# A message-passing kernel on one core: VectorE's edge loop written out for every iteration, and one wait per slot on GpSimd

## What is computed

```python
h = jnp.maximum(_layernorm(x), 0.0)
# node side: 32 scalars and 32 vectors of 3 per node, two small linear maps
sc_s, sc_v = fctp(x_s, x_v, sc_ws, sc_wv, MUL)
l1_s, l1_v = fctp(x_s, x_v, lin1_ws, lin1_wv, MUL)
# edge side
h = silu(rbf(d) @ fc_w1 / sqrt(8)); h = silu(h @ fc_w2 / 8)
w00, w01, w10, w11 = split(h @ fc_w3 / 8, 4)
gs, gv = l1_s[edge_src], l1_v[edge_src]          # the gather
o00 = w00 * gs * sh0;  o01 = w01 * gs * sh1
o10 = w10 * gv * sh0;  o11 = w11 * (gv . sh1) / sqrt(3)
agg = segment_sum(concat(...), edge_dst) / count  # the scatter
out = x + sc + tanh(agg_s @ alpha_w * ...) * lin2(agg)
```

## Time and profile before

| what | us |
|---|---|
| median of 3 runs | 2520.62 |
| lowest, highest | 2513.36, 2520.88 |
| span of the profiled execution | 2483.8 |
| time of the profiled execution itself | not given beside its span |
| PE busy | 1811.4 (73%) |
| DVE (VectorE) busy | 1783.0 (72%) |
| POOL (GpSimd) busy | 1578.4 (64%) |
| ACT (ScalarE) busy | 1199.1 (48%) |

### The profile page before, as it was taken

How to read it: one execution, slowest core, us unless ns; L and a number is a source line. 1 busy time by engine, 2 the same in 40 slices (tenths; PEclk the granted TensorE clock), 3 DMA queues, 4 the chain that set the end, 5 groups by cost and what they waited for, 6 DMA issues and landing times. The chain is left out here.

```text
span 2483.8 us, 34021 instructions
## 1 busy us (share of the span) xinstructions
PE 1811.4 (73%) x7969; PEld 1174.2 (47%) x7969; DVE 1783.0 (72%) x4669; ACT 1199.1 (48%) x3310; POOL 1578.4 (64%) x1624
## 2 busy tenths in 40 slices
PE   6577777787777777767677767667787776877777
PEld 6344444454444444444444434444554444544544
DVE  8577767767776777767676667767677776777777
ACT  6354545455454555444444344445444444445443
POOL 7566666666666666666666666666666666666563
PEclk9588878878888887788787878888888888888889
DMA  7322222222222222222122222222222222222222
GB/s 214 70 64 67 56 64 66 66 56 66 66 59 62 67 65 56 55 48 50 46 50 48 48 48 49 54 50 64 57 67 62 59 65 66 53 64 61 59 66 55
DMA packets 347699, 155.73 MB, mean 63 GB/s; under 512 B 237983, under 2 KB 322048, under 8 KB 347584
## 3 DMA queue, kind: packets, MB, share of 16 engines
q0 software_dynamic: 50016, 102.51, 15.7%
q1 hardware_dynamic: 296938, 51.75, 11.4%
q10 hardware_dynamic: 630, 0.29, 0.0%
HBM read 134.27 MB, written 20.15 MB: 62 GB/s over the span
## 5 line engine op out<-in xcount | busy, mean ns | idle before, releaser
L970 POOL DMA_INDIRECT lin_g<-lin_table,src_ix x1563 | 1530.0, 979 | 865.1 <-issue 441.5
L1157 ACT ACTIVATE lin_sh<-lin_g,harm 128x128 f32<-128x128 f32 x1563 | 483.8, 396 | 94.6 <-DMA lin_g<-lin_table,src_ix 87.6
L1040 PE MATMUL ps_sums<-near_sums,far_hot 128*128 128x257 f32 x520 | 208.0, 488 | 440.8 <-DVE agg L1474 206.0
L1030 PE MATMUL ps_near<-msg,onehot 128*64 128x257 f32 x3126 | 507.5, 471 | 1.2 <-DVE msg L1423 1.2
L1018 PE MATMUL ps_w<-w,h 128*128 128x256 f32 x1566 | 462.6, 440 | 28.2 <-ACT key_all L1167 18.5
L1018 PEld LDWEIGHTS ps_w<-w,h 128*128 128x128 f32 x1566 | 395.3, 272 | 135.4 <-issue 44.9
L999 PE MATMUL ps_h<-rbf,w 32*128 32x192 f32 x1044 | 277.0, 390 | 138.0 <-issue 67.1
L1415 DVE TENSOR_TENSOR msg<-lin_sh,key_all 128x576 f32<-128x576 f32 (+1 forms) x261 | 197.3, 756 | 249.9 <-ACT key_all L1167 209.5
L1167 ACT ACTIVATE key_all<-ps_w 128x768 f32<-128x768 f32 x261 | 213.5, 818 | 305.2 <-remote 188.6
L1030 PEld LDWEIGHTS ps_near<-msg,onehot 128*64 128x64 f32 x3126 | 241.3, 164 | 230.6 <-issue 175.7
L1383 DVE TENSOR_TENSOR lin_sh<-lin_g,ps_meta 128x576 f32<-128x576 f32 (+1 forms) x261 | 196.6, 753 | 212.2 <-DMA lin_g<-lin_table,src_ix 207.0
(11 more groups left out here) (175 smaller groups left out, 1655.2 us busy)
## 6 DMA issues: line engine op xcount, KB each, us to landing
lin_g<-lin_table,src_ix POOLq DMA_INDIRECT x1563
dist_in<-in_edge_weight SPq DMA_DIRECT2D x67, 96.0 KB
lin_table<-lin_out SPq DMA_DIRECT2D x24, 256.0 KB, 2.6
x_in<-in_x SPq DMA_DIRECT2D x24, 256.0 KB
skip_table<-x_in SPq DMA_DIRECT2D x24, 256.0 KB
xq<-in_x SPq DMA_DIRECT2D x23, 256.0 KB, 3.9
harm<-in_edge_attr SPq DMA_DIRECT2D x66, 48.0 KB
x_in<-skip_table SPq DMA_DIRECT2D x8, 256.0 KB
```

Source lines behind the costliest of these rows:

```text
L970: pool.indirect_dma_start(slot_tiles(s, u)[rows, t, :], None, lin_table, bass.IndirectOffsetOnAxis(ap=src_ix[rows, s.phase, u, col:col + 1 ...
L1030: mm = pe.matmul(ps_near[half * NEAR:(half + 1) * NEAR, 0:MSG + 1], onehot[:, u, t, :], msg[:, u % 2, t, :], start=(j == 0), stop=(j == PA ...
L1040: pe.matmul(ps_nodes(i), far_hot[:, u, :], near_sums[:, u % 2, :], start=True, stop=True).then_inc(sums_ready, 1)
L1157: last = act.activation(lin_sh0[:, u % 2, j, :], slot_tiles(s, u)[:, j, :], ACT.Copy, scale=harm[:, s.phase, u, harm_col(j):harm_col(j) + 1])
```

## The change

Two things. On VectorE the three hardware loops go; every iteration is written out with its number as a constant. Where the code told iteration 0 from the others by "the number is a constant", it now asks for the number 0. On GpSimd the three waits inside a group's gathers go; in their place is one wait before tile 0, for `msg_ready` of group n-4: VectorE has finished the message of the group that used the slot.

```diff
+            def first_turn(i):
+                return isinstance(i, int) and i == 0
...
-                return [(b, REST_ROWS[b]) for b in range(REST)] if isinstance(i, int) else [(b, P) for b in range(NB)]
+                return [(b, REST_ROWS[b]) for b in range(REST)] if first_turn(i) else [(b, P) for b in range(NB)]
...
-                                pool.wait_ge(near_ready, s.i * SLOTS + u - SLOTS + 1)
+                                pool.wait_ge(msg_ready, s.i * SLOTS + u - SLOTS + 1)
                                 pool.nop(nofuse=True)
...
-                            for k, t in enumerate(tiles):
-                                if not first and k == 2:
-                                    pool.wait_ge(h2_done, s.i * SLOTS + u)
-                                    pool.nop(nofuse=True)
-                                if not first and k == 4:
-                                    pool.wait_ge(sums_ready, s.i * SLOTS + u - SLOTS + 1)
-                                    pool.nop(nofuse=True)
+                            for t in tiles:
...
                         body(turn_of(0), share=True)
-                        with dve.Fori(0, STEPS // RING) as t:
-                            for k in range(RING):
-                                body(turn_in(t, 1, k), share=True)
-                        with dve.Fori(0, PLAIN // RING) as t:
-                            for k in range(RING):
-                                body(turn_in(t, 1 + STEPS, k))
-                        for i in range(1 + STEPS + PLAIN, EARLY0):
+                        for i in range(1, 1 + STEPS):
+                            body(turn_of(i), share=True)
+                        for i in range(1 + STEPS, EARLY0):
                             body(turn_of(i))
-                        body(turn_of(EARLY0), early=True)
-                        with dve.Fori(0, (EARLY - 1) // RING) as t:
-                            for k in range(RING):
-                                body(turn_in(t, EARLY0 + 1, k), early=True, finish=True)
+                        for i in range(EARLY0, ITERS - 1):
+                            body(turn_of(i), early=True, finish=i > EARLY0)
                         body(turn_of(ITERS - 1), finish=True, last=True)
```

More of the change, by code:

```diff
@@ L789, in gnn_kernel @@
             SKIP_STORES = 16 * (REST + STEPS)
+            def first_turn(i):
+                return isinstance(i, int) and i == 0
             def skip_rows(i):
-                return [(b, REST_ROWS[b]) for b in range(REST)] if isinstance(i, int) else [(b, P) for b in range(NB)]
+                return [(b, REST_ROWS[b]) for b in range(REST)] if first_turn(i) else [(b, P) for b in range(NB)]
             def skip_block(i, b):
-                return STEPS * NB + b if isinstance(i, int) else i * NB + (b - NB)
+                return STEPS * NB + b if first_turn(i) else i * NB + (b - NB)
             KEY_STEPS = HALVES
@@ L1459, in skip_sum @@
                             dve.wait_ge(sc_scaled, i + 1)
-                            for b, rows in skip_rows(i) if isinstance(i, int) else ():
+                            for b, rows in skip_rows(i) if first_turn(i) else ():
                                 last = dve.tensor_tensor(x_in[0:rows, b, :], ps_skip[0:rows, b * P:(b + 1) * P], x_in[0:rows, b, :], ALU.add)
-                            if not isinstance(i, int):
+                            if not first_turn(i):
                                 last = dve.tensor_tensor(x_in[:].rearrange("p b d -> p (b d)"), ps_skip[:], x_in[:].rearrange("p b d -> p (b d)"), ALU.add)
```

## The result

The changed kernel takes 2798.93 us (median of 4 runs, 2790.13 to 2799.64) against 2516.99 us: the ratio is 1.1114, with a 95% interval of 1.1088 to 1.114. The prediction was slower, 2595 us in a range up to 2770. The sign held, the size did not.

What follows compares the result with a forecast made beforehand. Waits were taken to bound the kernel: TensorE's signals held while GpSimd gathers. Span 2483.8 - 20 (loop) + 82 (longer stops) = 2546, plus 36.8 gives 2583, plus 13 for short cycles: 2595 us; range 2350 to 2770.

Steps and rivals of the forecast that it cites:

- The reading of "remote" and of the pauses: GpSimd's 325.1 us of "remote" waits: TensorE's semaphores are held during unbroken gathers and come through when GpSimd pauses long enough.
- The rival (a): Faster, 2397 us: GpSimd's pause and the signals' release merely coincide, since it waits for the same signals; chance of faster 0.39.
- The written-out loop at -20 us: VectorE's loops without branches back: at most 21 x 1.0 us saved in the late stretch, taken as 20, ends 0 and -63.
- That every trip would stall: VectorE's branches back: by the skill's fetch rule alone every trip stalls, up to 18 stalls; the trace has ten.
- VectorE's wait for gathers goes entirely: With gathers started early at the message, the 207.0 us that VectorE waits for gathers go.
- Next late are the weights: VectorE's next late input is ScalarE's copy of the weights, already 209.5 us of waits, which hangs on TensorE's signals.
- The sign that the wait before L1474 grows: On VectorE: if the forecast is right, its wait for ScalarE and its idle time before L1474 (188.0 us) grow.
- the cycle of three groups with a stop of 5.9 us: GpSimd runs three groups, then stops 5.9 us for a message: 28.4 us, 9.45 per group against 9.13, +82 us.
- Two groups are sure: Each GpSimd run gathers at least two groups: one message is just made, the next weights are mostly signalled.
- the tipping point: Between slower and faster: a GpSimd cycle of 5.9 / (9.13 - 7.5) = 3.6 groups per pause.
- Rival (b): Slower by more, 2839 us: GpSimd cycles of two groups, 10.45 us each, decide; chance 0.52 together with the forecast.
- The 36.8 us around the span: The earlier kernel's median stood 36.8 us above its profiled span; the forecast kept this, from 2546 to 2583 us.

Runs made afterwards that it cites:

- experiment 3: Changed kernel with GpSimd filling a private tile six times before the gathers of slots 0 and 2: 2622.92 us, 1.0414 of the kernel before.
- (4): Changed kernel with four such fills per stop, 2648.75 us; with two, 2772.88 us; with one small fill before each gather instead, 2755.62 us.
- experiment 5: Changed kernel gathering 32 numbers per row, 2818.1 us; 64 rows per gather, 2787.61 us; every second gather replaced by two fills, 2081.41 us.

## Why the prediction was right and wrong

- **The reading of "remote" and of the pauses** (TensorE's signals are held while gathers run on): right, and now shown by stops that are bound to nothing (experiment 3), by their length (4), and by spaced gathers (5). It was put too strongly in one point: a pause lets them through, but they can also come, late, with none. So it was at 1184.72 above, and in iteration 0 already: ScalarE got the weights at 96.81, while the gathers ran on until 98.50.
- **The rival (a)**, that stop and release coincide: refuted. It had 0.39, too much; iteration 0, where GpSimd waits for nothing, already spoke against it.
- **The written-out loop at -20 us**: ratio 0.9876 with the old waits is about 31 us, right in kind, a little small. In the changed kernel it is worth nothing; that the longer stops cover it is likely, not shown, and that the gain depends on the other half was not said. That every trip would stall does not follow from the rule as the prediction gives it: the loops have 17 taken branches, and the ten stalls are all those of the second and third loop, while the seven of the first leave VectorE idle for 1.0 to 1.1 us before L1474, against 0.6 at the other ends of iterations there.
- **VectorE's wait for gathers goes entirely**: right. **Next late are the weights**: right, 791.8 us. The sign that the wait before L1474 grows did not come: it fell from 190.7 us to 102.5.
- **The step that failed is the cycle of three groups with a stop of 5.9 us**, taken for the likeliest case: 9.45 us per group. Between 107.83 and 2754.99 the changed kernel makes its 64 iterations (rows below), 2647.2 us or 10.34 per group. That is near the 10.45 that I had priced for cycles of two groups, but partly by luck, for the cycles are mixed. With a pause counted from 1 us on, after iteration 0, the timeline has:

| gathers in a run | runs | mean pause behind it, us | mean cycle, us | us per group |
|---|---|---|---|---|
| 6 | 60 | 2.17 | 9.52 | 9.52 |
| 12 | 74 | 6.47 | 21.36 | 10.68 |
| 18 | 16 | 8.31 | 31.10 | 10.37 |

```profile
107.83 0.36 DVE L1333 SCALAR_TENSOR_TENSOR ps_meta<-dist_in,ps_meta 128x192 f32<-128x192 f32 x1
...
2754.99 0.36 DVE L1333 SCALAR_TENSOR_TENSOR ps_meta<-dist_in,ps_meta 128x192 f32<-128x192 f32 x1
```

- **In the sum:** (10.34 - 9.45) x 256 = 228 us more than forecast (28.4 / 3 is 9.47, a slip of 5 us); less the 13 already added for short cycles, plus the 20 of the loop that did not come, less 34 of the 36.8 below, is 201, against a miss of 204.
- Within the step three things were wrong. "Two groups are sure": 60 of the 150 runs had one. I argued that the longer stop lets the engines work ahead for a third group: only 16 runs had three. And where three groups do run, the stop is not 5.9 but 8.3 us on the mean, 8.9 in the timeline above, where the release came 3.2 us after 18 gathers and I had 1.8 from runs of twelve. So a cycle of three groups costs 10.4 us per group, hardly less than one of two, and at 8.3 us the tipping point, 8.3 / (9.13 - 7.5) = 5.1 groups, lies beyond the four slots.
- **Rival (b) had named the condition**: it tips when a signal is held from 7 us after a restart. The changed kernel's trace bears it out. Take TensorE's products at whose end ScalarE stood idle waiting for them. Of 196 that ended in the first 4 us of a run of gathers, none reached ScalarE more than 1 us late; of 89 in the next 2 us, 8 did; of 56 later ones, 29 did. A third group needs the signals of just that time.
- **The 36.8 us around the span** were a mistake of the same size as the gain of the loop: the changed kernel's median is 2.4 us above its span, the written-out loop's 2.3. Every timed execution of before on record is 1.8 us above its own span as well, so the profiled execution of before was simply a faster one. Against its own span the rate of before stays as read.
- **The range** ended some three quarters of the way from the forecast to the two-group cycle. Its two-group price, 2839, was closer than the forecast; with neither cycle resting on a row it should have been inside.

## What to carry to other kernels

When an engine waits and the profile names no instruction that has just ended, compare the moment of release with what a third engine does, GpSimd's indirect DMAs above all. A wait that looks superfluous may be what stops such a run in time: before taking it out, ask which signals it lets through, and what will end the stop that comes in its place. Price a cycle between engines from its two ends, and keep the worse one in the range unless a row excludes it.

## What the runs showed of the hardware

- While GpSimd issues indirect DMAs 1.25 us apart, TensorE's semaphores reach ScalarE late, by 16.3 us in the stop shown. In the changed kernel the delay depends on how long the run of gathers has gone on: over 1 us in 0 of 196 cases in its first 4 us, in 29 of 56 after 6 us. With the gathers spaced out (experiment 5) it was 1 of 681.
- In the stops shown the signals come 1.5 to 3.2 us after the last gather; now and then they come during the run (1184.72 above, after 11.6 us of waiting).
- A stop of 3.4 us let a signal through in 94 of 95 cases, one of 2.3 us in 66 of 88, one of 1.2 us in 15 of 81. Yet 1.2 us between any two gathers kept nearly all of them from being held.
- It depends neither on the bytes (2818.1 us with a quarter of them) nor, as far as one halving tells, on the rows (2787.61 us), nor on GpSimd's being busy (2081.41 us with fills between the gathers). Packets per gather stayed at 32 in all these runs, so whether they matter is untested, and what in the chip holds the signals was not found.
- Half the rows make a gather only 4% shorter (923 against 965 ns in the changed kernel).
- The mean granted clock went from 0.826 to 0.778, while TensorE's busy share fell from 73 to 67%. No run here separates its share in the time; in the stop shown above TensorE's weights were done at 1218.05, 13.3 us before ScalarE went on at 1231.36, so a faster clock would not have shortened that one.
- A taken branch back left VectorE idle for 5 to 7 us in ten of 17 cases (5.25 and 7.08 at the first of each loop). The Trainium skill, "Runtime: NRT & Kernel Launch", section "Instruction fetch mechanics", calls such a fetch a stall, and the trace agrees for those ten: at the first, transfers of instructions start at 1115.6 and 1118.0. The seven branches of the first loop left 1.0 to 1.1 us of idle time, 0.5 more than an iteration's end without a branch. Taking all branches out was worth 1.2%.
